# Last attention of a Flamingo block: head sums kept on partitions, denominators spread by DMA, projection started in the last unit

## The reference, cut to what matters

```python
qkv = (x @ W_qkv).reshape(Bx, Nx, 3, H, D)                # H = 16 heads, D = 16
q_n, qg_n = q / norm(q), q_g / norm(q_g)
sim = (qg_n * q_n).sum(-1).mean(-1)                       # then scaled to 0..1
pos = sim > 0.9
logits = einsum('bqhd,bkhd->bhqk', q * scale, k)
def masked_attn(tok_mask): ...                            # softmax over registers and one class of tokens
x_pos, x_neg = masked_attn(pos), masked_attn(~pos)
reg_out = (x_pos[:, :REG] + x_neg[:, :REG]) * 0.5         # REG = 5 register tokens
tok_out = where(pos, x_pos[:, REG:], x_neg[:, REG:])
out = concatenate([reg_out, tok_out]) @ W_proj + b_proj
x = x + tanh(g_ffn[1]) * out
```

## Time and profile before

| | us |
|---|---|
| runs | 1337.21, 1335.64, 1335.78; median 1335.78 |
| profiled execution, own time | 1333.82 |
| its span | 1332.1 |
| one unit of the last attention | 42.49 |
| busy: TensorE, VectorE, ScalarE, GpSimd | 1208.9, 1001.2, 835.0, 227.6 |
| mean granted TensorE clock | 0.968 |

### The profile page before, as it was taken

One profiled execution on the slowest core, in us unless ns is written; L12 is line 12 of the kernel. 1 busy time (PEld: TensorE's weight loads), 2 busy tenths in 40 slices (PEclk: granted clock), 3 DMA queues, 4 the chain that ended last, 5 costly groups with the idle time before them and its releaser, 6 DMA issues.

```text
span 1332.1 us, 26357 instructions
## 1 busy us (share of the span) xinstructions
PE 1208.9 (91%) x10562; PEld 559.8 (42%) x10562; DVE 1001.2 (75%) x1491; ACT 835.0 (63%) x1484; POOL 227.6 (17%) x176
## 2 busy tenths in 40 slices
PE   4888964999999999778999999999999999999988
PEld 2566753555566456243333232323233333332237
DVE  4895695665536768458999999999999999999702
ACT  1224673777743642115888878787787878887861
POOL 2130124554742423800000000000000000000000
PEclk8979996999999999888999999999999999999999
DMA  6100027566500334812424533244423444243003
GB/s 189 26 1 15 1 31 166 96 110 129 96 1 1 119 119 144 124 24 49 64 51 76 86 60 65 53 87 80 57 59 67 87 64 67 50 82 50 2 1 126
DMA packets 78825, 92.55 MB, mean 69 GB/s; under 512 B 15210, under 2 KB 53356, under 8 KB 78704
## 3 DMA queue, kind: packets, MB, share of 16 engines
q1 hardware_dynamic: 78704, 90.87, 34.5%
HBM read 67.02 MB, written 23.80 MB: 68 GB/s over the span
## 4 chain that ended last, share of the span: by engine, by line
PE 60%; DVE 29%; ACT 5%; issue 2%; DMA 1%; SPq 1%; POOL 1%; DVEq 0%; ACTq 0%; POOLq 0%
DVE sm L2083 19%; PE ps L1554 10%; PE ps L1545 9%; PE ps L1526 6%; ACT W L1021 3%; PE ps L1415 3%; PE ps L1321 2%; PE ps L1664 2%; PE ps L1312 2%; PE ps L1313 2%; PE ps L1374 2%; PE ps L1481 1%; PE ps L1536 1%; PE ps L1279 1%; PE ps L1277 1%
## 5 line engine op out<-in xcount | busy, mean ns | idle before, releaser
L2083 DVE TENSOR_REDUCE sm<-ps 128x1 f32<-128x1024 f32 x512 | 599.7, 1218 | 31.4 <-PE ps L1526 28.1
L1021 ACT ACTIVATE W<-ps 128x512 f32<-128x512 f32 x1024 | 534.8, 605 | 139.2 <-PE ps L1554 135.2
L1554 PE MATMUL ps<-R 99*32 99x512 bf16 x4096 | 317.8, 383 | 6.2 <-ACT W L1021 3.2
L1545 PE MATMUL ps<-W,R 128*32 128x512 f32 x2048 | 265.6, 594 | 0.7 <-ACT W L1021 0.7
L1554 PEld LDWEIGHTS ps<-R 99*32 99x32 bf16 x4096 | 86.3, 94 | 224.4 <-ACT W L1021 168.0
L803 POOL COPY R<-R 128x512 f32<-128x512 f32 x16 | 9.8, 613 | 633.1 <-PE ps L1545 633.1
L1526 PE MATMUL ps<-R 50*128 50x512 bf16 x512 | 89.1, 388 | 15.8 <-DVE sm L2083 13.1
L1526 PE MATMUL ps<-KM,R 50*128 50x512 bf16 x512 | 87.3, 384 | 9.6 <-DVE sm L2083 6.6
L945 ACT ACTIVATE R<-ps 77x512 f32<-77x512 f32 x128 | 75.1, 592 | 23.6 <-PE ps L1313 14.2
L1545 PEld LDWEIGHTS ps<-W,R 128*32 128x32 f32 x2048 | 63.1, 111 | 42.1 <-ACT W L1021 1.4
L1866 DVE TENSOR_REDUCE small<-ps 128x4 bf16<-128x308 f32 x128 | 57.5, 473 | 23.5 <-PE ps L1279 23.4
(11 more groups left out here) (262 smaller groups left out, 1565.3 us busy)
## 6 DMA issues: line engine op xcount, KB each, us to landing
R<-x_parts SPq DMA_DIRECT2D x96, 128.0 KB, 4.9
R<-q_parts SPq DMA_DIRECT2D x192, 64.0 KB
R<-q_parts SPq DMA_DIRECT2D x96, 128.0 KB
R<-k_parts SPq DMA_DIRECT2D x96, 128.0 KB
x_parts<-R SPq DMA_DIRECT2D x8, 768.0 KB, 6.8
q_parts<-R SPq DMA_DIRECT2D x24, 256.0 KB, 2.6
k_parts<-R SPq DMA_DIRECT2D x24, 256.0 KB, 2.6
X<-in_x SPq DMA_DIRECT2D x4, 1024.0 KB, 9.8
```

What stands on the lines that cost most here:

```text
L1021: act.activation(PR[:, s % 2, h, :], third_bank("score", 64 * u + n), ACT.Exp, scale=0.25).then_inc(s_sfree, 1)
L1545: mm = pe.matmul(bank(7)[32 * h:32 * h + 32, :], VST[j][:, k, h, :], PR[:, s % 2, h, :], start=(k == 0), stop=(k == TB - 1))
L1554: mm = pe.matmul(o[32 * c:32 * c + 32, :], KST[j][0:MAX_ROW + 1, h, t:t + 32], QST[j][0:MAX_ROW + 1, h, 512 * (s // 8):512 * (s // 8) + 51 ...
L2083: dve.tensor_reduce(MX[:, half, h, q:q + 1], bank(2 * ((p + 1) % 2), 2), AX, ALU.max).then_inc(s_tfree, 1)
```

## The change

The sums of a half stay as they are, with (head, channel) on partitions. Eight DMAs move them: four take each head's denominator row of 512 numbers to 32 partitions of 16 (`Rd2`), four take the 16 rows of each head to their place in `OT2`. VectorE inverts the denominators as 128x16, a DMA writes them to DRAM, another reads them back repeated over 16 partitions for each head (`Den2`), and GpSimd multiplies `OT2` by them. `OT2` already has the form that the projection needs as its weights, so the transposes of the tail and ScalarE's copies go. The projection of token tiles 0 to 13 is done one tile at a time behind each step of the last unit, tiles 14 to 31 after it. The register rows are summed and kept with channels on partitions, and averaged in two pieces: three batches ahead of the last unit, the last batch near the end. The attention's biases and the setup products of the second block use one semaphore where they used two. Nothing else is changed.

```diff
-        On2 = R1[:, :].rearrange("p (k u n) -> p k (u n)", u=UNITS, k=TB)
+        OT2 = R1[:, :].rearrange("p (j b t) -> p j b t", j=2, b=B)
+        Den2 = [W[:, 4096:4608], XNf[:, 1152:1664]]
+        Rd2 = sm2[:, 760:792].rearrange("p (u n) -> p u n", u=2)
...
-        PLAN[20].insert(0, ("out", 0))
-        PLAN[30].insert(0, ("out", 1))
-        PLAN_LAST = [[] for _ in range(32)] + [[("out", 1)]]
+        PLAN_LAST = [[] for _ in range(32)]
         PLAN_LAST[2].append(("rows", 1))
-        PLAN_LAST[20].append(("out", 0))
...
+            def sort_out(u, half):
+                b, rows, j = u // 4, 64 * (u % 2), u // 2 % 2
+                sp.wait_ge(s_oe2, 2 * u + half + 2)
+                for h in range(4):
+                    sp.dma_start(Rd2[32 * h:32 * h + 32, half, :],
+                                 Oe2[32 * h + 16:32 * h + 17, half, :].rearrange("p (a n) -> p a n", a=32)
+                                 ).then_inc(s_od2[half], 16)
+                for h in range(4):
+                    v = slice(rows + 16 * h, rows + 16 * h + 16)
+                    sp.dma_start(OT2[v, j, b, 512 * half:512 * half + 512],
+                                 Oe2[32 * h:32 * h + 16, half, :]).then_inc(s_od2[half], 16)
+
+            def spread_factors(u, half):
+                rows = 64 * (u % 2)
+                sp.wait_ge(s_rc2, B + 2 * u + half + 1)
+                if u >= 1:
+                    sp.wait_ge(s_dd2[half], 32 * u)
+                sp.dma_start(DR[half].rearrange("(p n) -> p n", p=P), Rd2[:, half, :]).then_inc(s_dd2[half], 16)
+                sp.wait_ge(s_dd2[half], 32 * u + 16)
+                if u >= 2:
+                    sp.wait_ge(s_nd2, 2 * (u - 2) + half + 1)
+                sp.dma_start(Den2[half][rows:rows + 64, :],
+                             DR[half].rearrange("(h n) -> h n", h=4).unsqueeze(1).to_broadcast([4, 16, 512])
+                             ).then_inc(s_dd2[half], 16)
...
             def body_sp(u, j, last=False, load=True):
                 store_row(j, 1, s_bfree, small_turn(u, "rows", 1) + 1, u)
                 if load:
                     load_max_stacks(u + 2, j)
+                if u >= 1:
+                    spread_factors(u - 1, 1)
+                sort_out(u, 0)
                 if not last:
                     store_row(1 - j, 0, s_bfree, small_turn(u, "rows", 0) + 1, u + 1)
+                spread_factors(u, 0)
+                if last:
+                    for c in range(3):
+                        store_out(c)
                 if load:
                     sp.wait_ge(s_sco, 64 * (u + 1))
                     load_stacks(u + 2, j)
+                sort_out(u, 1)
 
             for u in range(UNITS):
                 body_sp(u, u % 2, last=u + 1 == UNITS, load=u + 2 < UNITS)
+            spread_factors(UNITS - 1, 1)
+            for c in range(3, NC):
+                store_out(c)
...
-            for u in range(UNITS - 2):
-                pool.wait_ge(s_pv2, 2 + 16 * (u + 1))
-                stage_values(u + 2, u % 2)
+            def divide_out(u, half):
+                b, rows, j = u // 4, 64 * (u % 2), u // 2 % 2
+                v, n = slice(rows, rows + 64), 2 * u + half
+                pool.wait_ge(s_od2[half], 128 * (u + 1))
+                pool.wait_ge(s_dd2[half], 32 * (u + 1))
+                den = Den2[half][v, :]
+                o = OT2[v, j, b, 512 * half:512 * half + 512]
+                pool.tensor_tensor(o, o, den, ALU.mult).then_inc(s_nd2, 1)
+                pool.wait_ge(s_nd2, n + 1)
+
+            for u in range(UNITS):
+                divide_out(u, 0)
+                if u + 2 < UNITS:
+                    pool.wait_ge(s_pv2, 2 + 16 * (u + 1))
+                    stage_values(u + 2, u % 2)
+                    pool.wait_ge(s_vst, u + 3)
+                divide_out(u, 1)
...
             def copy_out2(u, half):
                 act.wait_ge(s_pv2, 16 * u + 8 * half + 10)
+                if u >= 1:
+                    act.wait_ge(s_od2[half], 128 * u)
                 act.copy(Oe2[:, half, :], bank(7)).then_inc(s_oe2, 1)
...
-                pe.matmul(bank(7)[0:REG, 0:C], Rsel, omk.rearrange("p j n -> p (j n)"),
-                          start=True, stop=True).then_inc(s_rsm, 1)
+                for j in range(2):
+                    mm = pe.matmul(bank(7)[:, REG * j:REG * j + REG], omk[:, j, :], Rsel, start=True, stop=True)
+                mm.then_inc(s_rsm, 1)
...
                     scores2(us, s, 3, js)
                     turns(plan[2 * n])
                     turns(plan[2 * n + 1])
+                    if last:
+                        project2(n)
                 if last:
                     values2(u, 15, j)
-                    turns(plan[32])
+
+            def project2(i):
+                c, q = i // 4, i % 4
+                n = NC + c
+                if i == 0:
+                    pe.wait_ge(s_tfree, PAIRS0 + 32 * (UNITS - 1))
+                    pe.wait_ge(s_avg, 2)
+                if i == 4 * (NC - 2):
+                    pe.wait_ge(s_avg, 4)
+                if q == 0 and c >= 2:
+                    pe.wait_ge(s_x3, n - 1)
+                o = bank(2 * (c % 2) + q // 2)[:, C * (q % 2):C * (q % 2) + C]
+                for j in range(2):
+                    mm = pe.matmul(o, OT2[:, j, c // 2, 512 * (c % 2) + P * q:512 * (c % 2) + P * q + P],
+                                   wproj[:, j, :], start=(q % 2 == 0 and j == 0), stop=(j == 1),
+                                   skip_group_check=True)
+                if q == 3:
+                    mm.then_inc(s_wo, 1)
...
+            for i in range(14, NT):
+                project2(i)
...
+            def invert_sums(u, half):
+                dve.wait_ge(s_od2[half], 128 * (u + 1))
+                dve.reciprocal(Rd2[:, half, :], Rd2[:, half, :]).then_inc(s_rc2, 1)
...
                     if what == "tile":
+                        if arg == 6 and u >= 1:
+                            invert_sums(u - 1, 1)
+                        if arg == 20:
+                            invert_sums(u, 0)
                         reduce_tile(n, PAIRS0 + 32 * u + arg, arg)
...
+            def average_registers(batches):
+                for j in range(2):
+                    o = OT2[:, j, batches, 0:REG]
+                    dve.scalar_tensor_tensor(o, o, 0.5, regT[:, j, batches, :], ALU.mult, ALU.add).then_inc(s_avg, 1)
+
+            def x4_chunk(c):
+                dve.wait_ge(s_wo, NC + c + 1)
+                dve.wait_ge(s_xb, B + c // 2 + 1)
+                xs = X[:, 4 * c:4 * c + 4, :]
+                dve.scalar_tensor_tensor(xs, bank(2 * (c % 2), 2).rearrange("p (i n) -> p i n", i=4),
+                                         gates[:, 3:4], xs, ALU.mult, ALU.add).then_inc(s_x3, 1)
+
             for u in range(UNITS):
+                if u + 1 == UNITS:
+                    dve.wait_ge(s_nd2, 8 * (B - 1))
+                    average_registers(slice(0, B - 1))
                 body_dve(u, last=u + 1 == UNITS)
...
+            x4_chunk(0)
+            invert_sums(UNITS - 2, 1)
+            invert_sums(UNITS - 1, 0)
+            for c in range(1, 3):
+                x4_chunk(c)
+            invert_sums(UNITS - 1, 1)
+            x4_chunk(3)
+            dve.wait_ge(s_nd2, 2 * UNITS)
+            average_registers(slice(B - 1, B))
+            for c in range(4, NC):
+                x4_chunk(c)
```

More of the change, by code:

```diff
@@ L362, in build_program @@
         s_krs = sem("k_residue")
-        s_kf = sem("k_copied")
         s_vf = sem("v_copied")
@@ L1045, in _ @@
                 body_act(u, last=u + 1 == UNITS)
-            for c in range(NC):
-                n = NC + c
-                act.wait_ge(s_onT, n + 1)
-                if c >= 2:
-                    act.wait_ge(s_wo, n - 1)
-                act.copy(OnT2[:, c % 2], bank(2 * (c % 2), 2).rearrange("p (j t) -> p j t", j=2)).then_inc(s_onc, 1)
         @block.tensor
@@ L1566, in turns @@
                             max_tile(p + arg, arg, jn)
-                        elif what == "rows":
+                        else:
                             o = take_third("small", small_turn(u, what, arg))
@@ L1570, in turns @@
                             max_rows(o, arg)
-                        else:
-                            out_turn(take_third("small", small_turn(u, what, arg)), arg, 2 * u + 2 + arg)
                 if not last:
@@ L2138, in _ @@
-            for c in range(NC):
-                dve.wait_ge(s_wo, NC + c + 1)
-                dve.wait_ge(s_xb2, c // 2 + 1)
-                xs = X[:, 4 * c:4 * c + 4, :]
-                dve.scalar_tensor_tensor(xs, bank(4 + 2 * (c % 2), 2).rearrange("p (i n) -> p i n", i=4),
-                                         gates[:, 3:4], xs, ALU.mult, ALU.add).then_inc(s_x3, 1)
+            x4_chunk(0)
[3 more added lines that the diff above has]
+                x4_chunk(c)
```

109 lines of the change are left out of this document (29 added, 80 removed).

## The result

The changed kernel takes 1371.97 us (median of four runs, 1368.28 to 1378.39) where the kernel before took 1335.71 beside it: a ratio of 1.0273, 95% interval 1.0246 to 1.0301. It is slower by 36 us, outside the range; the forecast, faster, was wrong. The profiled execution took 1378.39 us, 6.4 more than the median, with a span of 1376.7, and stands against 1333.82 and 1332.1 before.

What follows compares the result with a forecast made beforehand. It took TensorE and VectorE, handing each other maximum tiles, to bound the units, ScalarE the last unit, TensorE the tail. -27 + 3 + 8.5 - 19.3 - 1 = -35.8 gave a median of about 1300 us, range 1286 to 1322.

Steps and rivals of the forecast that it cites:

- Step 2: Units' new path: VectorE's reciprocal ahead of tile 20 waits about 0.2 us per unit for moves, +3 us (0 to 30).
- The 21 us of slack: SyncE's queue in a unit: slack in three pieces, the middle one, 7 us, to hold ten issues and a landing.
- step 1: Fifteen units lose their out turns, saving 1.8 us each: -27 us (-18 to -33).
- the moves are late in every unit: Rival, chance 0.26: VectorE stops 1 to 2 us ahead of tile 20 in each unit; 1320 us.
- The one for the other side: Rival, chance 0.04, slower than before: small moves' issues stop each unit; 0.76 us each turns the sign, 0.87 gives 1350.
- Step 3: Last unit takes in fourteen of 32 projection tiles, steps of 2.81 us: +8.5 us (+5.5 to +10).
- Step 4: Tail loses transposes, copies and 14 projection tiles, 24.2 us against 43.54: -19.3 us (-22 to -14).
- Step 5: Small edits: cheaper register sums -1 us (0 to -2), merged semaphores nothing.

Runs made afterwards that it cites:

- the floor run: Kernel before without the out turns of units 0 to 14 (transposes, reciprocals, multiplications left out), nothing added: 1307.81 us, ratio 0.979.
- the run with the round rearranged: Changed kernel with SyncE sending the second half's factors ahead of the maximum stacks, first half's moves after their first twelve loads: 1323.38 us, ratio 0.9906.

## Why the prediction was wrong

**Step 2 failed, "The new path, and the point where it bites".** It put +3 us where the kernel shows 15 x 5.08 = 76, far over its own upper bound of 30. The place was right, the reciprocal ahead of tile 20, and VectorE's arrival was right to 0.02 us. Of the terms of the moves' landing (23.2 forecast, 25.6 measured in the unit shown), the row's read-back went out at 5.1, where 3.3 to 4.5 was forecast, and the maximum stacks were out 0.5 later than its middle, since they took 0.7 less; the factors took 3.1 instead of 2.1; the eight moves 5.0 instead of 3.7, 0.62 each; the landing 1.4 instead of 1.7. The sum of these small misses, some 2.4, all falls on VectorE, since the slack had been used up to 0.2. That was the first error: a wait of +0.2 is the difference of two numbers near 23, each known to a microsecond or more on one side only, and it was read from favourable rows (a landing of 1.4, the median of the kernel before, and an issue of 0.46 for loads out of DRAM).

The second error is that the queue was followed once from row turn to reciprocal and not around its loop. By the prediction's own terms the second half's moves are issued by 0.4 ahead of the turn (loads from -10.2, 6.1 of issue, 3.7 for the moves), and SyncE is free for the row. The loads kept to that, 1028.20 to 1034.30, but the moves took 6.0, until 1040.37, 1.9 past the turn, and the row's write waited for them. SyncE has a closed path from the last scores of a unit to the reciprocal ahead of tile 20 of the next: 35.9 us from 1028.20 to 1064.06. From that reciprocal to the next last scores it is 8.8 us. Together 44.62, and that is the unit: 1028.20 to 1072.82, the same 44.62 as from row turn to row turn. SyncE is never idle on its part of the path but for the landings that it waits for. A stop doesn't buy SyncE time, because its own next round starts from scores that the stop has delayed. The 21 us of slack that the text counted in three pieces were of the whole round; on this path there was none. The runs bear this out from three sides: with no reader the same issues cost nothing (42.45), 3.1 us less on the path give 3.6 back (42.0), and with the path off SyncE the unit is 40.91, within 0.1 of the 40.9 (42.49 - 1.8 + 0.2) that was forecast. That it comes so close is in part chance, since step 1 holds two misses that cancel.

The third error is that a stop was priced at its own length. A third of the loss, 1.69 of 5.08 a unit, comes after it, TensorE at a granted clock of 0.52 and VectorE waiting for it. The lower clock level shows up in thirteen stretches of the units, 61 us in all, one behind each of the thirteen stops ahead of tile 20. The prediction kept the clock of the earlier trace rows everywhere.

**The rivals.** The one called "the moves are late in every unit" had the mechanism with half the size (1.5 a unit). The one for the other side, with a chance of 0.04 and 2.6 us a unit as the point where the sign turns, is what came: stops of 3.4 ahead of tile 20 in thirteen units. It asked for an issue of 0.76; 0.62 was enough, with the landings and the aftermath. Both belonged together as one case, and its chance was too small because the rows that spoke against it were of other transfers in a less crowded queue. The Trainium skill, "DMA: Bandwidth & Descriptors", section "Anatomy of one DMA", gives a fixed cost of about 2.0 us (for GpSimd's path), which the prediction set aside for the 1.4 of the earlier trace rows. The trace lies on both sides of it: 2.40 from the issue of a factor write to the DMA that waits for its landing (1054.64 to 1057.04), 1.46 half a unit later, 2.4 in the tail. By that figure the sum would have come out 14 us higher, at 1314, still on the wrong side.

**Step 1** (-27): right in its size, 28, by two misses that cancel. It took 2.1 a unit for the out turns less 0.3 for the reciprocals; the runs show 1.88 (the floor run) less nothing (units of 40.58 with the reciprocals, on GpSimd's queue, against 40.59).

**Step 3** (+8.5): right, +9.1; a step of 2.90 against 2.81. That interleaving doesn't pay was there to be seen in the prediction's own numbers: ten tiles, 8.65 us, were left to cover 12.5 of path, and 32 tiles in a row (27.7), the last addition and the store would have made a tail of 32.3, 8.1 over its 24.2, against 8.5 more in the last unit. Measured, it saved 2.0 in the tail (30.5 against 32.5) and cost 9.9 in the last unit (42.4 against 32.5).

**Step 4** (-19.3, -22 to -14): -13.0, just outside. The terms that were mis-sized, past the last values: reciprocal 7.0 (forecast 5.3), the write's landing 2.4 (1.6), the read and its landing 4.4 (2.5), so that chunk 6 starts at 17.0 (12.5); and chunks 6 and 7 take 8.83 (6.9), by the clock. GpSimd's multiplication was 1.26 (1.2). The sum itself was also short: from 0.64, step 2's own 3.7 and 1.7 give 6.0 for the landing and not 5.3, and 7.2 and 2.5 make 9.7 and not 9.5.

**Step 5** (-1): not confirmed, and too small to be seen. Up to unit 0 the changed kernel takes 1.9 more, 624.94 against 623.04, and its granted clock between 530 and 560 us was 0.66 against 0.83. Nothing points to the edits: the kernels above that keep them reach unit 0 at 621.25 to 625.80, and the floor run, which lacks them, at 625.26 with the same 0.66.

**What stays open.** How much of the 1.69 is the clock alone and how much the two engines getting back into step wasn't tried apart in the units; only in the tail was the clock tried by itself. Nor was it tried whether fewer loads, rather than another queue for the moves, would have given SyncE's round its slack back.

## What to carry to other kernels

When a wait for a queue's transfer is put in front of the engine that sets the pace, follow that queue once around its whole loop, from the event that starts its round through every landing that it waits for back to that event, and compare the loop's length with the period; slack that lies elsewhere in the round doesn't count. In these runs issues cost nothing until somebody waited behind them, so a step with waits of its own belongs in a queue whose other entries don't depend on it: here moving twenty small DMAs a unit from SyncE to GpSimd's queue turned +2.7% into -2.3%. Work that fills a stretch with idle time should first be asked what it was covering where it came from.

## What the runs showed of the hardware

- A move between two places in SBUF took SyncE's queue 0.62 us from one issue to the next (1057.68 to 1060.17, four), where the loads from DRAM beside it took 0.46 (5.58 for twelve). From GpSimd's queue it was 0.50 (2.02 for four). It isn't the shape alone: the row's write, 0.32 before, took 0.59 right behind the moves (1040.41). Issues also stretch behind stack loads, the last four moves of the half before to 3.51 and, in the unit from 1083.08, the twelve loads to 7.27; why isn't shown.
- A small DMA issued right behind the stack loads lands late. The 4 KB row took 1.4 us in the middle case before and takes 2.4 in the changed kernel, and in the run with the round rearranged eight moves landed 7.5 us after the last of them was issued, the DMA engines being fully busy (share 1.1) for the first three of them.
- The Trainium skill, "Trainium Kernel Development and Optimization", section "Key Constraints", says that issuing from several engines "only saves the sequencer's issue time". The runs agree, and show what that can be worth: 66 us, since what was saved included the waits in the sequence.
- TensorE's granted clock stood at 0.52 right behind 3.32 us in which it had worked 1.37, and at 1.00 four microseconds later. Sixteen products without a reader ahead of each of two projection tiles kept it at the upper level in the tail, which was 1.6 us shorter for it.
